# One layer of gated cross-attention and a quantised FFN: the first stage in a new order on each engine

## What is computed

```python
def channel_attention(q, k, v, scale):      # 4 heads of 128 channels
    scores = einsum('bhdn,bhen->bhde', qh, kh) * scale    # channels against channels
    return einsum('bhde,bhen->bhdn', softmax(scores), vh)

q = layernorm(x)
att = channel_attention(q*wqg+bqg, ctx*wkg+bkg, ctx*wvg+bvg) \
    + channel_attention(q*wql+bql, ctx*wkl+bkl, ctx*wvl+bvl)
x = x + tanh(g0) * (2*att*wp + bp)
def qlinear(x, w, b):       # scale = max|.| / 127 over the whole tensor, for x and w
    return (round(x/sx) @ round(w/sw).T + b) * (sw*sx)
h = gelu(qlinear(layernorm(x), w1, b1))     # 512 -> 2048
x = x + tanh(g1) * qlinear(h, w2, b2)       # 2048 -> 512
```

## Time and profile before

| | |
|---|---|
| median of 3 runs | 431.37 us (430.44 to 432.93) |
| the profiled execution, own time | 433.84 us |
| its span, first to last instruction | 432.0 us |
| granted TensorE clock, mean | 0.956 |
| busy: TensorE, VectorE, ScalarE, GpSimd | 384.8, 323.2, 270.6, 95.3 us |
| share of the chain that ended last: TensorE, VectorE, ScalarE | 65%, 15%, 6% |
| first stage; FFN product 1; product 2 | 0 to 174; 182 to 310; 319 to 428 us |

### The profile page before, as it was taken

One profiled execution on the slowest core, in us unless ns is written; L12 is line 12 of the kernel. 1 busy time (PEld: TensorE's weight loads), 2 busy tenths in 40 slices (PEclk: granted clock), 3 DMA queues, 4 the chain that ended last, 5 costly groups with the idle time before them and its releaser, 6 DMA issues.

```text
span 432.0 us, 6074 instructions
## 1 busy us (share of the span) xinstructions
PE 384.8 (89%) x2197; PEld 237.6 (55%) x2220; DVE 323.2 (75%) x574; ACT 270.6 (63%) x473; POOL 95.3 (22%) x170
## 2 busy tenths in 40 slices
PE   5779798797977978793999999999989999999996
PEld 5667667587766777542455445444644444444442
DVE  2775958858677566889989888987759768766662
ACT  1252749769697684370888788878789999540000
POOL 3354554655465130129300000000000000000000
PEclk9969789988998998987999999999999999999999
DMA  7999754665432111143467576100049999951222
GB/s 238 330 421 376 284 188 161 224 215 206 129 146 99 50 49 50 49 170 123 194 279 305 239 309 279 51 0 2 24 167 381 419 421 397 399 181 71 97 97 97
DMA packets 14813, 85.51 MB, mean 198 GB/s; under 512 B 1920, under 2 KB 2176, under 8 KB 5312
## 3 DMA queue, kind: packets, MB, share of 16 engines
q1 hardware_dynamic: 13840, 83.89, 50.9%
q10 hardware_dynamic: 944, 1.24, 1.1%
HBM read 55.77 MB, written 29.36 MB: 197 GB/s over the span
## 4 chain that ended last, share of the span: by engine, by line
PE 65%; DVE 15%; ACT 6%; issue 4%; DMA 4%; SPq 4%; POOL 0%; DVEq 0%; ACTq 0%; POOLq 0%
PE PS L1010 25%; PE PS L1042 25%; PE PS L859 5%; DMA X<-in_x 4%; PE PS L899 3%; DVE X L630 2%; DVE mxd L583 2%; DVE ring L720 2%; PE PS L972 2%; SPq L231 2%; DVE mid L569 2%; DVE w2q L623 2%; ACT ring L409 2%; ACT ring L453 1%; SPq L219 1%
## 5 line engine op out<-in xcount | busy, mean ns | idle before, releaser
L491 ACT ACTIVATE ring<-PS,bias,sc 128x512 f32<-128x512 f32 x128 | 97.2, 782 | 37.8 <-PE PS L1010 25.9
L1010 PE MATMUL PS<-mid,w1q 128*128 128x512 bf16 x500 | 113.6, 386 | 1.8 <-DVE mid L736 1.1
L1042 PE MATMUL PS<-w2q,w1q 128*128 128x512 bf16 x501 | 110.1, 379 | 2.0 <-DVE w1q L803 0.9
L1010 PEld LDWEIGHTS PS<-mid,w1q 128*128 128x128 bf16 x512 | 50.5, 100 | 62.0 <-issue 4.8
L1042 PEld LDWEIGHTS PS<-w2q,w1q 128*128 128x128 bf16 x512 | 49.9, 98 | 61.9 <-DVE w1q L803 1.4
L749 DVE TENSOR_REDUCE hmax<-ring 128x1 f32<-128x2048 f32 x30 | 68.0, 2280 | 7.6 <-ACT ring L491 7.6
L510 ACT ACTIVATE ring<-ring,sc 128x2048 f32<-128x2048 f32 x31 | 59.5, 1995 | 8.7 <-DMA ring<-spilled_hidden 8.7
L803 DVE TENSOR_SCALAR w1q<-ring 128x2048 bf16<-128x2048 f32 x31 | 37.9, 1224 | 24.9 <-PE PS L1042 21.5
L859 PE MATMUL PS<-ring 128*128 128x129 f32 x256 | 38.1, 320 | 14.9 <-DVE X L630 14.9
L859 PEld LDWEIGHTS PS<-ring 128*128 128x128 f32 x256 | 37.0, 234 | 15.9 <-issue 15.9
L845 PE MATMUL PS<-ident 128*128 128x128 f32 x240 | 33.9, 305 | 5.4 <-POOL ident L306 3.4
(11 more groups left out here) (103 smaller groups left out, 393.8 us busy)
## 6 DMA issues: line engine op xcount, KB each, us to landing
spilled_hidden<-ring SPq DMA_DIRECT2D x20, 1024.0 KB, 3.9
ring<-spilled_hidden SPq DMA_DIRECT2D x20, 1024.0 KB, 8.7
ring<-in_ctx SPq DMA_DIRECT2D x8, 1024.0 KB, 7.9
ring<-in_ctxT SPq DMA_DIRECT2D x8, 1024.0 KB, 4.8
X<-in_x SPq DMA_DIRECT2D x7, 1024.0 KB, 11.9
out<-X SPq DMA_DIRECT2D x7, 1024.0 KB, 10.3
ring<-in_w1T SPq DMA_DIRECT2D x4, 1024.0 KB, 12.8
ring<-in_w2T SPq DMA_DIRECT2D x8, 512.0 KB, 3.3
```

Source lines behind the costliest of these rows:

```text
L491: nc.scalar.activation(ring[:, s * CH + c, (h % CH) * N:(h % CH + 1) * N], PS[:, hidden_bank(s, h), :], ACT.Gelu, scale=S1, bias=bias1[:, ...
L1010: mm = nc.tensor.matmul(PS[:, hidden_bank(s, h), :], w1v[:, k, h * P:(h + 1) * P], xqT[:, s, k, :], start=(k == 0), stop=(k == NH - 1))
L1042: mm = nc.tensor.matmul(PS[:, par * NT + i, :], hq[:, c, k, i * P:(i + 1) * P], w2v[:, kk, :], start=(kk == 0), stop=(kk == KH - 1))
```

## The change

It touches the first stage and the seam. Line numbers of the diff are those of the files before and after; the file after is 31 lines longer.

- *ScalarE*: in a turn now weights_out(b), left_rows(b+1), local_out(b), normalise(b+2), exponentials(b+1), squares(b). `quantise_w1` is gone from it. After normalise(0) it makes W2o from PSUM, after exponentials(0) bvb and bp.
- *VectorE*: statistics(b+2), in the turns of b = 0 and 1 one w1 max (parts 2 and 3), largest_square(b-1), columns(b+1), ..., scores(b+1), then three additions, reciprocals(b+1), the fourth addition. `w1_scale` follows the scores. statistics(1) and w1_max(0) stand before the loop, w1_max(1) behind the scores of batch 0.
- *GpSimd*: `quantise_w1(b-2)` after key_sum(b+2); at the seam it starts on w2 only when x of batch 1 is quantised, and on the second half when x of batch 2 is.
- *TensorE*: three matmuls spread the rows wkg, wkl, bp from one partition, in place of two broadcast loads (512 and 256 KB). In group 0 of product 1, w2's maximum is turned at tile 12 instead of 8, and x of batch 1 at tile 14 instead of 12.
- *SyncE*: w1 parts come between x and k of batches 0 to 2; the first ctxT follows the last w1 part.

```diff
@@ -106,0 +107,2 @@
+        row_vectors = sq_sb[0:1, 0:3, :].rearrange("p i d -> p (i d)")
+        ones = cut(P)
@@ -246,0 +250 @@
+            load_w1(0)
@@ -248,3 +252 @@
-            load_cT(0)
-            for k in range(NH):
-                load_w1(k)
+            load_w1(1)
@@ -252 +254,3 @@
-            load_cT(1)
+            load_w1(2)
+            load_w1(3)
+            load_cT(0)
@@ -254,0 +259 @@
+            load_cT(1)
@@ -301,0 +307 @@
+            nc.gpsimd.memset(ones, 1.0).then_inc(ones_ready, 1)
@@ -355,0 +362,8 @@
+            def quantise_w1(q):
+
+                pool.wait_ge(w1_step, 8)
+                w = w_stage[:, q * PW:q * PW + PW]
+                nc.gpsimd.tensor_scalar(w, w, ISW1, MAGIC, ALU.mult, ALU.add).then_inc(w1y_done, 1)
+                pool.wait_ge(w1y_done, q + 1)
+                nc.gpsimd.tensor_scalar(w1q[:, q * PW:q * PW + PW], w, -MAGIC, 1.0, ALU.add, ALU.mult).then_inc(w1q_done, 1)
+
@@ -360,0 +375,4 @@
+                if 2 <= b < B:
+                    quantise_w1(b - 2)
+                if b == B - 1:
+                    quantise_w1(B - 2)
@@ -362,0 +381,2 @@
+                if b == B - 1:
+                    quantise_w1(B - 1)
@@ -374,0 +395,4 @@
+                if n == 0:
+                    pool.wait_ge(xq_done, 8)
+                if n == 2:
+                    pool.wait_ge(xq_done, 12)
@@ -386 +410 @@
-            act.dma_start(wk_rows.rearrange("p j e -> p (j e)"), wk.to_broadcast([P, 2 * D])).then_inc(wk_in, 16)
+            act.dma_start(row_vectors, rows).then_inc(rows_in, 16)
@@ -389 +412,0 @@
-            act.dma_start(bpt, bp.to_broadcast([P, D])).then_inc(bp_in, 16)
@@ -412,6 +434,0 @@
-            def quantise_w1(q):
-                w = w_stage[:, q * PW:q * PW + PW]
-                nc.scalar.activation(w, w, ACT.Copy, scale=ISW1, bias=MAGIC).then_inc(w1y_done, 1)
-                act.wait_ge(w1y_done, q + 1)
-                nc.scalar.activation(w1q[:, q * PW:q * PW + PW], w, ACT.Copy, bias=-MAGIC).then_inc(w1q_done, 1)
-
@@ -456,0 +474,6 @@
+            act.wait_ge(cols_in, 16)
+            act.wait_ge(spread_done, 1)
+            for g in range(2):
+                for h in range(NH):
+                    nc.scalar.activation(W2o[:, NH * g + h, :], PS[:, 2 + g, h * P:(h + 1) * P], ACT.Copy,
+                                         scale=WQ[g][:, h:h + 1]).then_inc(scaled, 1)
@@ -459,0 +483,5 @@
+            for g in range(2):
+                nc.scalar.activation(bvb[:, NH * g:NH * g + NH, :],
+                                     BV[g].rearrange("p (h r) -> p h r", r=1).to_broadcast([P, NH, P]),
+                                     ACT.Copy).then_inc(scaled, 1)
+            nc.scalar.activation(bpt, psC, ACT.Copy, scale=tg[:, 0:1]).then_inc(scaled, 1)
@@ -461,2 +488,0 @@
-                if b >= 1:
-                    squares(b - 1)
@@ -467,2 +492,0 @@
-                if b + 1 < B:
-                    exponentials(b + 1)
@@ -471,6 +495,3 @@
-                if b == 1:
-                    act.wait_ge(w1_step, 8)
-                if b >= 1:
-                    quantise_w1(b - 1)
-            squares(B - 1)
-            quantise_w1(PIECES - 1)
+                if b + 1 < B:
+                    exponentials(b + 1)
+                squares(b)
@@ -530,0 +552 @@
+                        wait(dve, aggr_done, 4 * b)
@@ -550,0 +573,2 @@
+                if b == 0:
+                    dve.wait_ge(scaled, 2 * NH)
@@ -613,0 +638 @@
+                dve.wait_ge(scaled, 2 * NH + 3)
@@ -626 +651 @@
-            def add_product(b):
+            def add_product(b, tiles):
@@ -628 +653 @@
-                for i in range(NT):
+                for i in tiles:
@@ -636,7 +660,0 @@
-                dve.wait_ge(wk_in, 16)
-                for g in range(2):
-                    for h in range(NH):
-                        j = NH * g + h
-                        V.tensor_scalar(W2o[:, j, :], wk_rows[:, j, :], WQ[g][:, h:h + 1], None, ALU.mult)
-                    V.tensor_copy(bvb[:, NH * g:NH * g + NH, :],
-                                  BV[g].rearrange("p (h r) -> p h r", r=1).to_broadcast([P, NH, P]))
@@ -646,2 +663,0 @@
-                dve.wait_ge(bp_in, 16)
-                V.tensor_scalar(bpt, bpt, tg[:, 0:1], None, ALU.mult)
@@ -652,0 +669,2 @@
+            statistics(1)
+            w1_max(0)
@@ -654 +671,0 @@
-            dve.wait_ge(setup, 1)
@@ -656 +673 @@
-                if b + 2 < B:
+                if 0 <= b and b + 2 < B:
@@ -657,0 +675,8 @@
+                if b == 0:
+                    w1_max(2)
+                if b == 1:
+                    w1_max(3)
+                if b >= 1:
+                    largest_square(b - 1)
+                if b == B - 1:
+                    w2_max(0)
@@ -662,3 +686,0 @@
-                if b == B - 1:
-                    largest_square(b - 1)
-                    w2_max(0)
@@ -668,2 +689,0 @@
-                if b == 1:
-                    w1_scale()
@@ -672,7 +692,5 @@
-                if b in (-1, 0):
-                    w1_max(2 * b + 2)
-                    w1_max(2 * b + 3)
-                if 1 <= b < B - 1:
-                    largest_square(b - 1)
-                if b + 1 < B:
-                    reciprocals(b + 1)
+                if b == -1:
+                    w1_max(1)
+                    reciprocals(0)
+                if b == 1:
+                    w1_scale()
@@ -680 +698,4 @@
-                    add_product(b)
+                    add_product(b, range(NT - 1))
+                    if b + 1 < B:
+                        reciprocals(b + 1)
+                    add_product(b, range(NT - 1, NT))
@@ -753,0 +775 @@
+            quantise_x(1, 1, 0)
@@ -766 +788,3 @@
-                if not last:
+                if g == 1:
+                    group_max(g, s, 0)
+                if g > 0 and not last:
@@ -768 +792,2 @@
-                group_max(g, s, 0)
+                if g != 1:
+                    group_max(g, s, 0)
@@ -895,0 +921 @@
+                pe.wait_ge(scaled, 2 * NH + 3)
@@ -921,0 +948,5 @@
+            pe.wait_ge(ones_ready, 1)
+            pe.wait_ge(rows_in, 16)
+            for n, bank in enumerate((2, 3, 7)):
+                mm = nc.tensor.matmul(PS[:, bank, :], ones[0:1, :], row_vectors[:, n * D:(n + 1) * D], start=True, stop=True)
+            mm.then_inc(spread_done, 1)
@@ -935,0 +967 @@
+                    pe.wait_ge(scaled, 2 * NH)
@@ -997 +1029 @@
-                    if g == 0 and h == KH // 2:
+                    if g == 0 and h == 3 * KH // 4:
@@ -1002 +1034 @@
-                    if h == 3 * KH // 4 and not last:
+                    if h == (KH - 2 if g == 0 else 3 * KH // 4) and not last:
```

20 lines of the change are left out of this document (10 added, 10 removed).

## The result

The changed kernel took 407.92 us (median of 4 executions, 407.38 to 410.12), the kernel before 430.90 beside it (429.38 to 432.93): ratio 0.947, 95% interval 0.942 to 0.952. **Faster, by 5.3%.** The forecast was 404.8, range 398.5 to 413. The profiled execution took 408.44 us, and its span went from 432.0 to 406.6.

The account below looks back on a forecast made before the run. A chain across engines, last ScalarE's normalise before the gram, was taken to bound the first stage. Gains 12.1 + 5.0 + 0 + 2.0 + 7.5 = 26.6 gave 407.2 us profiled, 404.8 median, range 398.5 to 413.

Parts of the forecast that it names:

- start: Up to the gram of batch 2: fewer broadcasts and earlier loads of x bring minus 5.0 us, bounds 0 and 8.
- batch 1's turn: First stage, turn of batch 1: 19.3 us against 19.6, counted as 0, bounds -0.3 and +1.6.
- steady turns: First stage, batches 2 to 6: idle before the gram goes, turns of 14.25 us, together minus 12.1 us.
- last turn: End of the first stage: additions come ahead of the squares and w2 maxima, minus 2.0 us.
- V: In a turn of the first stage, the end of a value product, from which the forecast counts its times.
- Both waits end within 2.5 us of each other, so undoing one alone would bring little: Steady turn, before the gram: ScalarE's exponentials then normalise, and VectorE's squares maximum then additions; undoing one brings little.
- GpSimd takes w1 for nothing: First stage: quantising w1 moves from ScalarE to GpSimd, 2.1 us a piece, and costs 0.
- the ring: w1 piece, w2 and k loads, key sums on GpSimd: 13.5 us, costs 0; as rival 15.2, 407.7, chance 0.12.
- The prediction's sign of being wrong: First stage, GpSimd: the prediction is wrong if key sums wait for k.
- Hidden under the wait for x and k: Start: the three matmuls spreading the weight rows, and their scaling on ScalarE, cost no time.
- Seam -7.5: Between first stage and FFN: x quantised earlier with GpSimd held back, minus 7.5 us, bounds -4 and -9.
- The rival's four slow grams: First stage, TensorE: the clock stays low, four grams of 5.45 us, total 411.4 us, chance 0.15.

Follow-up runs that it names:

- Run 3: Changed kernel with VectorE's maximum of squares behind columns and products instead of ahead of them: 404.57 us, ratio 0.943.
- run 6: Changed kernel with VectorE's old order (maximum of squares between scores and additions, all four additions behind the reciprocals): 408.53 us, ratio 0.945.
- run 5: Changed kernel with ScalarE's old order, exponentials before normalise: 417.94 us, ratio 0.967.
- run 1: The changed kernel again, unaltered, as base of the first group: 406.26 us, ratio 0.944.
- run 4: Changed kernel with w1's scale ahead of the scores and the maximum of squares behind columns and products: 401.97 us, ratio 0.935.
- run 10: The kernel of run 9 with each SyncE load of w2 behind the next load of k: 399.96 us, ratio 0.924.
- run 12: The kernel of run 8 with GpSimd held back until x of group 1 is quantised: 412.10 us, ratio 0.951.
- Run 2: Changed kernel with w1's scale read ahead of the score tiles of batch 2: 404.83 us, ratio 0.943.
- Run 11: Changed kernel with the start's order of loads and VectorE's maxima of w1 as before, weight rows still spread by TensorE: 408.81 us, ratio 0.946.
- run 7: Changed kernel with the pieces of w1 quantised on ScalarE again, behind the squares: 415.26 us, ratio 0.960.
- run 8: Changed kernel with the seam as before, x of batch 1 quantised after w2's scale and GpSimd not held back: 416.46 us, ratio 0.962.
- run 9: The kernel of run 4 with w2's first maximum moved behind the last value weights: 401.88 us, ratio 0.928.

## Why the prediction was right, and where it was not

The time lies 3.1 over the forecast and inside the forecast's own range (400 to 409). Against the profiled execution it was forecast at 407.2 and took 408.44. The other 1.9 us of the miss come from the step to the median: the old profile lay 2.5 over its median, the new one only 0.5. The sum came nearer than its terms, which is in part luck: start and batch 1's turn brought 2.4 less than forecast and the steady turns 0.7 less, the last turn 1.6 more. By its terms:

- **Steady turns: right** (-12.1 forecast, -11.4 measured). The next thing late was the one named. Its size was off, 1.02 instead of 0.6: the columns came 6.4 after V, not 6.2, and TensorE was ready at 5.6. Run 3 took it away and three turns fell to 13.7.
- **"Both waits end within 2.5 us of each other, so undoing one alone would bring little": wrong for one of them.** Beside the pieces of w1 on GpSimd, run 6 has ScalarE's order alone and keeps the whole gain; run 5 has VectorE's alone and keeps 2.7 us of the steady turns' 11.4. Two waits that end close together are no tie when only one of them comes last every time: behind ScalarE's, VectorE's left 0.72, and mending that cost 1.02 elsewhere.
- **GpSimd takes w1 for nothing: right.** A piece took 1.11 + 1.05, the forecast 2.1. The Trainium skill, GPSIMD Engine Reference, section Key points, has elementwise work at about half VectorE's speed; that would have been an estimated 3.8 a piece, and the trace disagrees for these passes with one input. With two inputs a ratio near two does show: 1.27 us for GpSimd's first key sum (L336) against 0.69 for VectorE's constant row (L641), both 128x512. The ring did not bind at 14.37. In the first trace the last three loads of k landed in 8.1, 6.7 and 6.4 us, near the forecast's 7.5. In run 1 they took 7.9, 9.0 and 8.7, where the prediction's sum for the ring comes to about 15, and the turns stayed 14.37. The prediction's sign of being wrong, key sums that wait for k, came (0.54, in run 1 up to 2.55) and cost nothing: over three loads there was more room than that sum gives. Runs 3 and 4, with turns under 14, ran into the ring, and run 10 cut it.
- **Start -5.0 and batch 1's turn 0: their sum was off by 2.4**, and batch 1's +3.3 lies outside its bounds (-0.3 to +1.6). The order of events came as the term had it: two maxima ahead of the columns (8.0 after V = 44.42, forecast 8.2), scores behind them, the scale behind the scores. What failed is the clock in that stretch. After the idle 2.63 the constant sums (L925) took 3.06, against 1.99 to 2.05 in later turns, so scores began at 57.89, 13.5 after V and not 12.5. After the idle 2.68 the ones rows took 2.09 and not 1.0, the product 5.61 and not 3.8. Together some 3.9 for the 22.93 - 19.3 = 3.6 that were missing. My bound had the low clock for the product alone. How much it costs is a draw: in run 1 the constant sums took 1.95 behind the same idle time, and in run 12, with a product of 4.48, the turn was 20.5 and the gram of batch 3 started at 64.87, just where the forecast has it (69.92 - 5.0). Run 2 takes out the wait for the scale (turn -2.2 against run 1); in runs 4 and 10 the turn is 16.7.
- **"Hidden under the wait for x and k" was wrong for the spreading matmuls.** They end at 10.2 in the first trace, and the first gram starts at 15.92 instead of 14.19; a maximum of w1 on VectorE, which ends at 19.84, covers that. At 5.48 us they are not covered, and the start is 2.1 longer (run 1).
- Run 11 shows what neither term said: the new loads and places of w1's maxima bring nothing as they stand, since the 3.2 us that they win are lost in the next turn. The net -2.6 of the two terms is all there in run 11, within the spread of these traces, so it comes from what run 11 keeps: the broadcasts that are gone, the statistics of batch 1 ahead of the loop, the new orders. Which of them was not run; nor whether the early loads pay with the order of run 10, whose turn of batch 1 is short.
- **Last turn -2.0: mechanism right, one part missing.** To value product 7 it came to -1.9. The other -1.8 is nearly all that product itself: 3.81 where it had taken 5.40. I had written that from there nothing is touched; shorter waits touched the clock. The waits ahead of it were 2.54 and 2.10, and are 1.18 and 1.59. In the runs with the shorter pair it always took 3.81, and in run 7, with 2.72 and 0.84, it took 5.21.
- **Seam -7.5: right** (-7.7; by run 8 the old seam costs 6.6 in this kernel's trace, 6 to 8 by the ratios). Run 12 shows the reason given for it to be the right one.
- **The clock.** With the waits gone the grams run at full clock, as forecast. The rival's four slow grams did not come; but the clock took its share where waits remained, as above.

## What to carry to other kernels

When two engines' waits end close together, find which one comes last in every turn, and mend that one alone first; the other may be no more than a wait that moves. Follow a gain past the place where it is made before you book it: in the start some 3 us were won and lost again within 20 us, the moved maximum of run 9 won 0.8 and lost it within 16 us, and the 3.8 of run 12's hold were 2.1 one group later. And compare more than one trace where the clock has a say. And when turns get shorter, ask again about each ring through a DMA queue: a load written behind another that waits for an engine inherits that wait.

## What the runs showed of the hardware

- **GpSimd beside VectorE.** VectorE's passes from SBUF to SBUF with one input (128x512 fp32) took 0.48 us each alone (1.91 for four) and 1.70 beside GpSimd's (6.80; 6.71 in run 12). Its copies out of PSUM (1.27 for two in run 8, beside GpSimd) and its maxima (4.46 for two) did not stretch. The Trainium skill, SBUF — State Buffer, section "SBUF: two separate sides", says that certain VectorE instructions and GpSimd share a port pair which one holds for a whole instruction; by that rule, the trace agrees. Runs 8 and 12 give the price: with GpSimd beside the passes TensorE waits 6.96 for them, with GpSimd held back 0.57.
- **GpSimd and ScalarE are equal on a quantising piece**: 1.11 + 1.05 against 1.14 + 1.06 us over 128x1024.
- **The same stretch at two clocks.** The changed kernel's first trace and run 1 are one program, with the same idle times of 2.63 and 2.68 us in batch 1's turn. Behind the first, TensorE's constant sums took 3.06 us in one (granted clock 0.62) and 1.95 in the other (1.00). Behind the second, the value product took 5.61 and 5.64, and 4.48 in run 12, the same program up to there. Behind the idle time of 1.02 in the steady turns nothing was slow. A wait of 2 to 3 us is a chance of the low clock, not its price, and a forecast should carry that as a range.
- **Matmuls over one partition at two speeds.** The three that spread a row (1x512, fp32) took 2.84 to 3.17 us in eight traces and 5.48 or 5.49 in five, at a granted clock of 1.00 by the profile of run 1. The cause is open.
